# All rows gathered by GpSimd in a graph layer: the one-hot fetch is taken out, and each half's gathers wait for the other half's landing

## The reference

```
h = x[src]                                   # (103125, 64)
for r in range(16):
    m += (etypes == r)[:, None] * (h @ w[r])
out = segment_sum(m, dst, 3125)
return layernorm(x + out)                    # over the 64 features
```

## Time and profile before

| | us |
|---|---|
| median of 3 timed runs | 767.06 (766.12 to 768.82) |
| profiled execution, span from first to last instruction | 1331.0 |
| TensorE busy in the profiled execution | 905.4 |
| VectorE busy | 656.1 |
| ScalarE busy | 628.9 |
| GpSimd busy | 553.1 |

### The profile page before, as it was taken

One profiled execution on the slowest core, in us unless ns is written; L12 is line 12 of the kernel. 1 busy time (PEld: TensorE's weight loads), 2 busy tenths in 40 slices (PEclk: granted clock), 3 DMA queues, 4 the chain that ended last, 5 costly groups with the idle time before them and its releaser, 6 DMA issues.

```text
span 1331.0 us, 25286 instructions
## 1 busy us (share of the span) xinstructions
PE 905.4 (68%) x8746; PEld 801.7 (60%) x8747; DVE 656.1 (49%) x2201; ACT 628.9 (47%) x1217; POOL 553.1 (42%) x591
## 2 busy tenths in 40 slices
PE   4576686766766768676675857667676766767676
PEld 3465575665656657566565756557575655756575
DVE  7653644545545364453635445363544545354444
ACT  6455453553544535444453535445363444535442
POOL 5643534444434353343534344352533435344341
PEclk9687887877868688686887778786787778788676
DMA  6211211111111111111111111121111111111111
GB/s 166 54 45 37 53 40 39 42 46 42 43 36 46 33 51 42 38 45 34 49 40 41 38 41 43 34 51 28 53 41 36 45 34 51 35 44 43 28 28 35
DMA packets 29901, 58.93 MB, mean 44 GB/s; under 512 B 11656, under 2 KB 11906, under 8 KB 29882
## 3 DMA queue, kind: packets, MB, share of 16 engines
q0 software_dynamic: 18464, 37.85, 11.0%
q1 hardware_dynamic: 11264, 20.41, 5.8%
q10 hardware_dynamic: 154, 0.42, 0.1%
HBM read 56.23 MB, written 2.40 MB: 44 GB/s over the span
## 4 chain that ended last, share of the span: by engine, by line
PE 66%; issue 30%; ACT 2%; DVE 1%; DMA 0%; ACTq 0%; DVEq 0%
PE own L767 48%; PE agg L805 11%; PE rel L818 6%; ACT pick L426 1%; DVE outT L647 0%; DMA x_sb<-in_x 0%; ACT away L420 0%; PE rel L825 0%; PE own L915 0%; DVE x_sb L681 0%; ACT rows L436 0%; DVE xp L558 0%; PE own L748 0%; ACT idx L451 0%; DVE outT L622 0%
## 5 line engine op out<-in xcount | busy, mean ns | idle before, releaser
L767 PE MATMUL own<-xp,pick 125*128 125x192 bf16 x5725 | 653.5, 271 | 377.6 <-issue 371.3
L767 PEld LDWEIGHTS own<-xp,pick 125*128 125x128 bf16 x5725 | 545.9, 108 | 474.6 <-issue 458.6
L345 POOL DMA_INDIRECT rows<-x_parts,gidx x558 | 529.5, 949 | 612.5 <-ACT gidx L379 231.1
L539 DVE TENSOR_SCALAR pick<-src_h,node 125x516 bf16<-125x516 f16 (+1 forms) x1220 | 459.7, 456 | 291.5 <-ACT src_h L387 290.3
L435 ACT ACTIVATE rows<-own 128x384 bf16<-128x384 f32 x122 | 57.4, 470 | 643.0 <-remote 581.2
L622 DVE TENSOR_TENSOR outT<-outT,rel 64x32 f32 x124 | 22.3, 180 | 361.6 <-PE rel L825 349.2
L420 ACT ACTIVATE away<-src_h,node_neg 125x516 bf16<-125x516 f16 (+1 forms) x305 | 192.5, 693 | 7.6 <-PE own L767 5.9
L426 ACT ACTIVATE pick<-away,one 125x516 bf16<-125x516 bf16 (+1 forms) x305 | 192.0, 696 | 0.0
L805 PE MATMUL agg<-onehot,rows 128*128 128x112 bf16 x2418 | 167.9, 243 | 15.8 <-issue 15.6
L805 PEld LDWEIGHTS agg<-onehot,rows 128*128 128x128 bf16 x2418 | 163.7, 117 | 18.3 <-issue 18.1
L605 DVE TENSOR_SCALAR onehot<-ramp,krel 128x112 bf16<-128x112 bf16 x806 | 148.9, 262 | 6.6 <-PE agg L805 6.6
(11 more groups left out here) (67 smaller groups left out, 83.0 us busy)
## 6 DMA issues: line engine op xcount, KB each, us to landing
src_b<-in_src SPq DMA_DIRECT2D x61, 258.0 KB
rows<-x_parts,gidx POOLq DMA_INDIRECT x577
x_parts<-xp SPq DMA_DIRECT2D x1, 728.0 KB
x_parts<-xp SPq DMA_DIRECT2D x1, 672.0 KB
out<-x_sb SPq DMA_DIRECT2D x2, 224.0 KB
x_sb<-in_x ACTq DMA_DIRECT2D x1, 364.0 KB
x_sb<-in_x SPq DMA_DIRECT2D x1, 336.0 KB
src_i<-in_src SPq DMA_DIRECT2D x1, 312.0 KB
```

The source lines that it names most:

```text
L345: pool.indirect_dma_start(rows[:, u, j, :], None, x_parts, bass.IndirectOffsetOnAxis(ap=gidx[:, u, j:j + 1], axis=0)).then_inc(rows_in[u] ...
L539: v.tensor_scalar(pick[u][:, b, 0:CUT * cut_width(u, odd)], src_h[u][:, :, 0:cut_width(u, odd)], node[:, b:b + 1], None, ALU.is_equal).the ...
L767: return nc.tensor.matmul(own_slot(u, h), pick[u][:, b, h * P:(h + 1) * P], xp[:, b, 0:SPLIT, :].rearrange("p s d -> p (s d)"), start=(b = ...
```

## The change

The whole one-hot fetch goes: the broadcasts on SyncE with their waits, the narrowing and the picks on ScalarE, the picks on VectorE, the products on TensorE, the copies into `rows`, their buffers, semaphores and the two constants `node` and `node_neg` that GpSimd made. GpSimd gathers all 13 tiles of every half with line 345. Before the gathers of a half it waits, besides the two waits that it had, for `late_in` of the other half. With one way of fetching left, odd and even turns are alike. The semaphore `rows_in[u]` now counts ten tiles of a half, and the aggregation waits for it before its first tile; the order of what is left on each queue stays as it was.

The diff, cut to its core (what is left out is the removal of the functions named above, of their calls, buffers and semaphores):

```diff
@@ group_loop
-                body(i, i % 2 == 1)
+                body(i)
             with eng.Fori(1, LAST // 2) as k:
-                body(k * 2, False)
-                body(k * 2 + 1, True)
+                body(k * 2)
+                body(k * 2 + 1)
@@ gpsimd
-            def fetch(i, u, odd):
+            def fetch(i, u):
                 if not is_first(i):
                     pool.wait_ge(agg_ready[u], i)
                 pool.wait_ge(gidx_ready[u], i + 1)
+
+                if u == 1:
+                    pool.wait_ge(late_in[0], (i + 1) * (16 * (GT - LATE)))
+                elif not is_first(i):
+                    pool.wait_ge(late_in[1], i * (16 * (GT - LATE)))
                 pool.nop(nofuse=True)
-                if not has_own(i, u):
-                    for j in range(FEWER):
...
-                if own_count(u, odd) == FEWER:
...
-                for j in range(OWN[u], GT):
+                for j in range(GT):
                     pool.indirect_dma_start(
                         rows[:, u, j, :], None, x_parts,
                         bass.IndirectOffsetOnAxis(ap=gidx[:, u, j:j + 1], axis=0)).then_inc(rows_in[u] if j < LATE else late_in[u], 16)
@@ scalar
+            def turn(i, more=True):
                 if not is_first(i):
                     take_agg(i - 1, 1)
                     take_rel(i - 1)
                 if more:
                     group_indices(i + 1, 0)
                 take_agg(i, 0)
                 if more:
                     group_indices(i + 1, 1)
@@ tensor, aggregate
-                if has_own(i, u):
-                    pe.wait_ge(own_rows[u], (own_turns(i, u) + 1) * 4)
-                else:
-                    pe.wait_ge(first_in, 16 * FEWER)
                 for j in range(GT):
-                    if j == FEWER and own_count(u, odd) == FEWER:
-                        pe.wait_ge(fourth_in, (i // 2 + 1) * 16 if isinstance(i, int) else (i + 2) * 8)
-                    if j == OWN[u]:
-                        pe.wait_ge(rows_in[u], (i + 1) * (16 * (LATE - OWN[u])))
+                    if j == 0:
+                        pe.wait_ge(rows_in[u], (i + 1) * (16 * LATE))
                     if j == LATE:
                         pe.wait_ge(late_in[u], (i + 1) * (16 * (GT - LATE)))
```

More of the change, by code:

```diff
@@ L125, in gnn_resnorm @@
         onehot = sb("onehot", [P, 2, GT, KEYS], bf16)
[L126 to L131, removed]
         one = sb("one", [NP, 1])
@@ L199, in group_loop @@
             for i in range(first, 2):
-                body(i, i % 2 == 1)
+                body(i)
             with eng.Fori(1, LAST // 2) as k:
-                body(k * 2, False)
-                body(k * 2 + 1, True)
+                body(k * 2)
+                body(k * 2 + 1)
             if last > LAST:
[L205 to L231, removed]
+                body(LAST)
         def y_bank(n):
@@ L298, in _ @@
             sp.dma_start(par_row[:, :], par[:, :]).then_inc(par_in, 16)
-            group_loop(sp, turn, first=2)
             with go_general(sp):
@@ L347, in fetch, with turn @@
                         bass.IndirectOffsetOnAxis(ap=gidx[:, u, j:j + 1], axis=0)).then_inc(rows_in[u] if j < LATE else late_in[u], 16)
-            def turn(i, odd):
-                fetch(i, 0, odd)
-                fetch(i, 1, odd)
+            def turn(i):
+                fetch(i, 0)
+                fetch(i, 1)
             group_loop(pool, turn)
@@ L532, in _ @@
             v = nc.vector
-            def picks(i, u, odd):
-                dve.wait_ge(src_h_ready[u], own_turns(i, u) + 1)
-                if not first_own(i, u):
-                    dve.wait_ge(own_done[u], own_turns(i, u) * 2)
-                for b in range(VPICK):
-                    v.tensor_scalar(pick[u][:, b, 0:CUT * cut_width(u, odd)], src_h[u][:, :, 0:cut_width(u, odd)], node[:, b:b + 1], None, ALU.is_equal).then_inc(pick_ready[u], 1)
             steps = [0]
@@ L560, in _ @@
             v.tensor_copy(src_f[:, :], src_i[:, :]).then_inc(src_cast, 1)
-            dve.wait_ge(const_set, 5)
-            picks(0, 0, False)
+            dve.wait_ge(const_set, 3)
             dve.wait_ge(dst_in, 64)
@@ L596, in _ @@
                             shift[:, :].rearrange("g (j o) -> g j o", o=1).to_broadcast([G, GT, P]), ALU.subtract).then_inc(krel_cast, 1)
-            picks(1, 0, True)
             dve.wait_ge(krel_done, 2)
@@ L650, in _, with turn @@
             dve.wait_ge(out_zeroed, 1)
-            def turn(i, odd, more=True):
-                if is_first(i):
-                    pass
-                elif more:
-                    picks(i + 1, 0, not odd)
-                else:
+            def turn(i, more=True):
+                if not more:
                     dve.wait_ge(again_done[0], 1)
@@ L662, in turn @@
                     onehots(i, 1)
-                if not is_first(i):
                     add_rel(i - 1)
                 if more:
-                    picks(i + 1, 1, not odd)
                     onehots(i + 1, 0)
@@ L673, in _ @@
                             AX.X, ALU.max).then_inc(any_set, 1)
-            turn(LAST, False, more=False)
+            turn(LAST, more=False)
             def finish(n):
@@ L750, in edge_transposes @@
                 last.then_inc(done, 1)
[L752 removed]
+            pe.wait_ge(const_set, 3)
             pe.wait_ge(src_cast, 1)
             edge_transposes(src_f, own[0:2], srcT_done)
[L756 to L779 removed]
             def window_starts(i, u):
@@ L835, in transpose_x @@
                 pe.wait_ge(x_centered, 2)
-                for u in range(2):
-                    pe.wait_ge(own_rows[u], (own_turns(LAST, u) + 1) * 4)
                 for n in range(n0, n1):
@@ L844, in transpose_x, with turn @@
                     last.then_inc(xT_done, 1)
-            def turn(i, odd, more=True):
-                if has_own(i, 1):
-                    fetch_own(i, 1, odd)
+            def turn(i, more=True):
                 if is_first(i):
                     pe.wait_ge(par_in, 16)
-                    aggregate(i, 0, odd, window_starts(i, 0))
-                    fetch_own(i + 1, 0, not odd)
-                    aggregate(i, 1, odd, window_starts(i, 1))
+                    aggregate(i, 0, window_starts(i, 0))
+                    aggregate(i, 1, window_starts(i, 1))
                     pe.wait_ge(w_centered, 2)
@@ L856, in turn @@
                 relate(i - 1)
-                aggregate(i, 0, odd, window_starts(i, 0))
+                aggregate(i, 0, window_starts(i, 0))
                 turn_rel(i - 1)
-                if more:
-                    fetch_own(i + 1, 0, not odd)
-                else:
+                if not more:
                     transpose_x(0, 3)
-                aggregate(i, 1, odd, window_starts(i, 1))
+                aggregate(i, 1, window_starts(i, 1))
                 if not more:
```

108 lines of the change are left out of this document (3 added, 105 removed).

## The result

| | before | after |
|---|---|---|
| median of the timed runs, us | 767.94 (4 runs, 766.12 to 769.04) | 1174.51 (4 runs, 1174.28 to 1175.31) |
| ratio after / before | | 1.530 (1.528 to 1.533) |
| span of the profiled execution, us | 1331.0 | 1172.5 |
| GpSimd busy, us | 553.1 | 768.2 |
| TensorE busy, us | 905.4 | 357.4 |

The account below looks back on a forecast made before the run. GpSimd's gathers were taken to pace the kernel, TensorE close behind. 19.2 + 2.1 + 1006.3 - 0.3 + 103.7 + 21.0 + 2.0 = 1154.0 us, plus 3.8 missed before: forecast 1158 us, range 1065 to 1195.

Parts of the forecast that it names:

- The pace: Whole kernel before: GpSimd's 577 gathers at 1.2485 us plus both ends make 763.3 us, against 767.06 measured.
- rival (a): Every gather: the pause is partly the recorder's, TensorE bound the kernel before; about 1047 us at 1.10 us each; chance 0.22.
- The sum for TensorE: Kernel before: products, aggregation matmuls and relation stages make 676 us; with start and end some 50 us short of GpSimd.
- The added gathers: GpSimd's queue: 229 more gathers, 806 instead of 577, at 1.2485 us each, add 285.9 us.
- The new wait: GpSimd at 61 half ends: a pause of 2.0 us in place of 0.30, 103.7 us in all.
- the bound of 3.5 us a boundary: Upper bound at half ends, from one trace boundary of 3.51 us: 3.2 us more each, 196 us in all.
- rival (b): Half ends: the wait costs nothing, hidden or already met, only the added gathers count; 1054 us; chance 0.05.
- rival (c): Half ends: each of 61 boundaries costs 3.51 us instead of 2.0; 1250 us; chance 0.07.
- The end: Behind the last gather: the same chain, 21.0 us, plus 2.0 us for TensorE's clock at 0.50.
- fast rival (d): Every gather: without the picks' VectorE load gathers get cheaper, faster than before, 508 us or 734 us; chance 0.03.
- The remainder: Whole kernel: the 3.8 us the rebuilt sum missed on the kernel before, carried over into the forecast.
- The profile to come: Profile after: 806 gathers, about 66% of span, GpSimd as chain's engine, TensorE under a third, span within 2% of timed.

Follow-up runs that it names:

- The run with an input of one run of 516: Changed kernel with 20 useless tensor_scalar of 125 x 516 added on VectorE per round, input one gapless run instead of three of 172: 1353.97 us, ratio 1.762.
- the run with `tensor_tensor`: Changed kernel with two useless two-input fp32 tensor_tensor of 62 x 1664 added behind every round of line 454: 1354.54 us, ratio 1.765.

## Why the prediction was right, and where it was off

**The pace.** The step that decided was to read a kernel whose profile calls TensorE the chain as paced by GpSimd, because 577 spacings of 1.2485 us and the two ends gave the timed 767 us to 3.8 us. Two runs confirm it from both sides: a fifth fewer products for TensorE leave the time at 768.13 us, 62 gathers less take 25 us off. The rival (a), a gather cheaper than recorded, falls with them and with the profile after, where the span is the timed time. The sum for TensorE was some 20 us too low (it had no hand-overs), so GpSimd's lead was 25 us and not 50. That doesn't enter the forecast.

**The added gathers.** Predicted 229 x 1.2485 = 285.9 us; the run without the wait gives 285.3 us. For all 806, without what the half ends cost on top: predicted 1006.3 + 2.1 - 0.3 = 1008.1 us, measured 762.8 + 226.7 + 61 x 0.305 = 1008.1 us. That they agree to the digit is chance. The two lines 443 and 445 (the former 593 and 595) fell on the first three gathers, 1.12, 1.43 and 1.62 us long, 1.3 us more than usual where 2.1 were expected; and one more, 1.51 us, lies beside line 481 in the last turn.

**The new wait.** This is the term that was mis-sized: 2.0 us at an end predicted, 2.31 us measured, 61 x 0.31 = 18.9 us. It has two parts, the landing and the wake-up, the time from a release to the start of the gather. The wake-up was right (0.73 us forecast; here the gather starts at 567.26, 0.73 us behind the landing below). The landing was read as the last start of a packet, 1.25 to 1.3 us. But packets that have ended are not yet a semaphore at its full count. Windows behind the gather that ended at 564.98 (length, busy of five engines, clock, DMA share, GB/s):

```profile
565.90:566.30 0.40, 0.10 (x2) 0.00 (x0) 0.00 (x0) 0.00 (x0) 0.00 (x0) 0.50 0.12 41
566.30:566.70 0.40, 0.04 (x1) 0.04 (x2) 0.00 (x0) 0.05 (x1) 0.00 (x0) 0.50 0.00 0
```

The last packets start before 566.30, as before, and the waiting ScalarE starts at 566.65. The page's 2.5 us from issue to landing, less the gather's 0.945, put the full count at 1.55 us; 1.55 + 0.73 is 2.28. None of the rows read from the trace of before had an engine that waited for a landing with nothing else late; the bound of 3.5 us a boundary did hold the number. The error lies in how the trace was read, not in the kernel: the same 2.32 us stand in the kernel before with the wait put in.

**Whether another wait hides it.** That none does was right: rival (b), 1054 us, is what the run without the wait gives (1053.64), not the change. That the boundary isn't 3.5 us (rival (c)) was right too.

**The end.** 23.0 us predicted behind the last gather, 22.6 measured, and this is luck. The granted clock was 0.50 nearly throughout, as said, but it had risen by the last relation stage: 16 matmuls in 1.94 us, not 3.36, so most of the 2.0 us booked for the low clock didn't come. In their place TensorE stood longer before the last transposes, 3.65 us instead of 2.01 (the second and the third line, after and before; start, length, idle before):

```profile
1154.05 1.94 PE L629 MATMUL rel<-w_pair,aggT 128*128 128x64 f32 x16
...
1160.31 5.14 PE L717 MATMUL own<-ident,outT 64*125 64x64 f32 x21 [3.65 <-issue]
...
1318.80 5.16 PE L915 MATMUL own<-ident,outT 64*125 64x64 f32 x21 [2.01 <-DVE outT L622]
```

**The fast rival (d) and the rule behind it.** That the picks' removal gives GpSimd nothing was right; the run with work of their form put back shows it. The reason given was wrong. The prediction set the rule of the Trainium skill against the picks in the earlier trace rows and said that here it is the other way about. The run with an input of one run of 516 shows the rule at work, by 4.9 us in each of 37 bursts of 60; the picks escape it by their form. Two-input operations hold a gather up as well, which the trace showed and the run with `tensor_tensor` confirms.

**The remainder.** 2.0 us lie between span and timed median, 3.8 us had been carried over. Together: 1158 + 18.9 - 0.4 - 1.8 = 1174.7 us, against 1174.51.

**The profile to come.** 806 gathers, 66% of the span, 744 short and 61 long pauses, TensorE under a third and a span near the timed time came as said. The chain of the page, which was to show GpSimd, did not: it broke off.

## What to carry to other kernels

When a profiled span is far above the timed runs, take only durations and undisturbed spacings from it, rebuild each engine's time from them, and see which sum closes with the timed runs: the engine with the smallest busy share was the pace here, since its fixed pauses don't count as busy. Work moved to an engine that already paces costs its full price (229 gathers, 285 us), and the relief of the others was worth nothing. A wait for the landing just issued cost the issuing engine 2.3 us instead of 0.3; waiting for a transfer three gathers earlier, or for the buffer and the indices alone, cost nothing.

## What the runs showed of the hardware that was not expected

- An indirect gather costs GpSimd 0.945 us busy and 0.305 us until the next for 128 rows of 512 bytes, and 0.906 us busy for 64 rows: almost all of it is per gather, whatever its rows (32 packets in both).
- VectorE's one-source 16-bit operations leave the gathers alone with an input of three runs of 172 (0.95 us beside 20 of them). With one run of 516, 37 of 60 bursts held a gather to their end (5.5 to 6.2 us); in the other 23 the gathers kept their 0.94 us and the burst took 6.2 us instead of 5.3. Two operations with two fp32 inputs from SBUF held a gather up in all of 60 rounds (3.4 to 4.6 us).
- A loop body of four turns instead of two came with 123 instruction packets instead of 19, and with pauses of TensorE of up to 3.8 us, 38.8 us in all.
- The profile of before was stretched by 564 us, with gaps of a microsecond between ready matmuls, and those of kernels with nearly the same instructions weren't: 25224 instructions in a span of 740.8 us with a timed 743.35. What stretched that one execution stays open.
